# Attention 0: value product one unit later with two buffers, and each unit's last projection copied one unit later on ScalarE

## The reference

```python
def _L0_attn_ref(x, w_qkv, w_out):
    H, D, window_size = (16, 64, 32)
    xn = rms_norm(x)
    qkv = xn @ w_qkv.T
    ...
    q = apply_rope(q, cos, sin)
    k = apply_rope(k, cos, sin)
    attn = jnp.einsum('bhqd,bhkd->bhqk', q, k) * scale
    mask = (q_pos >= k_pos) & (q_pos - k_pos <= window_size)
    attn = jnp.where(mask[None, None], attn, NEG)
    attn = jax.nn.softmax(attn, axis=-1)
    out = jnp.einsum('bhqk,bhkd->bhqd', attn, v)
    ...
    return out @ w_out.T

h = _layernorm(x, axis=-1) * (1 + ca) + sa
x = x + ga * _L0_attn_ref(h, L0_attn_w_qkv, L0_attn_w_out)
```

## Time and profile before

| | us |
|---|---|
| Median of 3 runs (1296.6 to 1300.16) | 1297.09 |
| Profiled execution, first to last instruction (span) | 1295.1 |
| What lies between this span and that median | 2.0 |
| PE busy in the span | 975.8 |
| DVE busy | 805.3 |
| ACT busy | 639.2 |
| POOL busy | 430.4 |
| Attention 0's first and last y_mul, start | 121.5, 599.5 |

### The profile page before, as it was taken

One profiled execution on the slowest core, in us unless ns is written; L12 is line 12 of the kernel. 1 busy time (PEld: TensorE's weight loads), 2 busy tenths in 40 slices (PEclk: granted clock), 3 DMA queues, 4 the chain that ended last, 5 costly groups with the idle time before them and its releaser, 6 DMA issues. The chain is left out here.

```text
span 1295.1 us, 25137 instructions
## 1 busy us (share of the span) xinstructions
PE 975.8 (75%) x8604; PEld 662.5 (51%) x8604; DVE 805.3 (62%) x1683; ACT 639.2 (49%) x2132; POOL 430.4 (33%) x332
## 2 busy tenths in 40 slices
PE   6779998989899999985613769747348787867665
PEld 3456565656656565664503556534225454545454
DVE  5777758687777767564657514112136878559995
ACT  3565767767676767671101323112038777643322
POOL 2334333333342423321000857886611312200221
PEclk9789899999999998987555789888759999868967
DMA  6564343434443434431402123445310000000000
GB/s 198 150 182 107 92 123 88 119 96 113 102 113 100 113 83 107 104 91 42 102 0 62 45 59 69 61 73 129 31 66 1 1 2 1 1 1 9 17 17 25
DMA packets 89009, 93.62 MB, mean 72 GB/s; under 512 B 18800, under 2 KB 62304, under 8 KB 88944
## 3 DMA queue, kind: packets, MB, share of 16 engines
q1 hardware_dynamic: 78576, 84.12, 24.7%
q0 software_dynamic: 10368, 8.66, 4.7%
HBM read 24.36 MB, written 10.70 MB: 27 GB/s over the span
## 5 line engine op out<-in xcount | busy, mean ns | idle before, releaser
L835 POOL TENSOR_TENSOR qk_cos<-qk_raw,const 128x512 f32<-128x512 f32 x128 | 183.2, 1432 | 313.0 <-ACT qk_raw L589 313.0
L575 ACT ACTIVATE prob<-psS,neg_max 128x96 f32<-128x96 f32 x512 | 167.9, 342 | 86.5 <-DVE neg_max L670 85.7
L442 PE MATMUL psQ<-a_xnT,weights 128*128 128x512 f32 x250 | 146.0, 668 | 2.1 <-ACT a_xnT L621 1.4
L550 PEld LDWEIGHTS psO<-probT,v_windows 96*64 96x64 f32 x2048 | 73.7, 143 | 142.6 <-ACT probT L649 121.1
L550 PE MATMUL psO<-probT,v_windows 96*64 96x64 f32 x2048 | 91.8, 235 | 43.9 <-ACT probT L649 43.9
L685 DVE TENSOR_TENSOR qk_roped<-qk_cos,qk_swapped 128x512 f32<-128x512 f32 x128 | 119.0, 929 | 5.9 <-DVE qk_swapped L676 5.5
L1508 POOL DMA_INDIRECT sums<-ex_y,ex_index x64 | 97.6, 1525 | 39.5 <-issue 23.5
L1497 POOL DMA_INDIRECT ex_rows<-rows,ex_index x64 | 67.1, 1048 | 121.8 <-DMA ex_index<-lists 102.6
L575 ACT ACTIVATION_READ_ACCUMULATOR prob<-psS,neg_max 128x1 f32 x512 | 105.4, 206 | 0.0
L1442 ACT ACTIVATE ex_hidden<-ex_psH,ex_b 128x512 f32<-128x512 f32 x64 | 43.7, 687 | 114.4 <-PE ex_psH L1401 59.7
L649 ACT COPY probT<-psT 96x512 f32<-96x512 f32 x128 | 76.8, 600 | 46.5 <-PE psT L530 46.5
(11 more groups left out here) (317 smaller groups left out, 1936.2 us busy)
## 6 DMA issues: line engine op xcount, KB each, us to landing
qk_swapped<-qk_raw SPq DMA_DIRECT2D x512, 64.0 KB, 2.0
v_windows<-v_tok SPq DMA_DIRECT2D x32, 384.0 KB, 4.4
v_windows<-v_tok SPq DMA_DIRECT2D x32, 256.0 KB, 3.6
mod<-mod_rows SPq DMA_DIRECT2D x12, 512.0 KB, 6.0
ex_w<-in_L_ffn_W SPq DMA_DIRECT2D x16, 256.0 KB
v_windows<-v_tok SPq DMA_DIRECT2D x32, 96.0 KB, 2.1
...
```

The lines of the kernel that those rows point to most:

```text
L442: last = nc.tensor.matmul(bank, k.wqkvT[:, col:col + P], xnT[:, :], start=True, stop=True)
L550: ins = nc.tensor.matmul(psO[D * j:D * j + D, i * P + a * HALF:i * P + (a + 1) * HALF], vw[:, par, a, t, hd], probT[:, 2 * j + i, a * HALF ...
L575: last = nc.scalar.activation(prob[:, s, 2 * j + i, :], psS[:, s, j, i * KW:(i + 1) * KW], ACT.Exp, bias=nmax[:, s, 2 * j + i:2 * j + i + ...
L835: nc.gpsimd.tensor_tensor(rcos[:, half, :], raw[:, half, :], k.const[:, K_COS:K_COS + T], ALU.mult).then_inc(cos_done, 1)
```

## The change

PE runs O one unit late: `apply(b, u-1)` stands in unit u, before the second projection (in unit 8 before the first). probT has two buffers; O in unit u waits for the probT of unit u-1 and for the copy of the O of unit u-2. ACT copies oT of unit u-2, then probT(u), then the **last** projection of the unit before (`late`), then runs the exps, then copies the unit's other projection where it has two. v has two buffers, and the semaphore of the windows is split in two; SP issues `windows(g+1)` at t = 1 behind the swap, waiting for the value products of the quad before. The last two pairs of the output projection move into the next sequence's unit 0, behind its T, and the copy of xnT from the end of unit 7 to the middle of unit 8. The modulation weights of layer 0 use memory of mod1. DVE's and POOL's bodies are not changed.

```diff
--- before.py
+++ after.py
@@ -116,7 +116,8 @@
         sb = lambda name, shape: ctx.enter_context(nc.sbuf_tensor(f"m_{name}{layer}", shape, F32))
         sem = lambda name: ctx.enter_context(nc.semaphore(f"m_{name}{layer}"))
         self.c, self.ex, self.si, self.siT = sb("c", [B, C]), sb("exp", [B, C]), sb("silu", [B, C]), sb("siluT", [C, B])
-        self.w, self.sgn, self.mag = sb("w", [C, MODS * C]), sb("sign", [B, C]), sb("mag", [B, C])
+        self.w = sb("w", [C, MODS * C]) if layer else k.mod1[:, 0, 0:MODS, :].rearrange("p b c -> p (b c)")
+        self.sgn, self.mag = sb("sign", [B, C]), sb("mag", [B, C])
         self.rows, self.n = k.mod_rows_sb[layer], 0
         self.ld, self.exped, self.chain, self.multiplied, self.siT_ready, self.rows_ready, self.rows_stored = (
             sem(n) for n in ("ld", "exped", "chain", "multiplied", "siT", "rows", "rows_stored"))
@@ -333,9 +334,9 @@
         junk, ms, mse, rms = sb("a0_squares", [P, TILES, C]), sb("a0_ms", [P, TILES]), sb("a0_mse", [P, TILES]), sb("a0_rms", [P, TILES])
         raw, swp, rcos = (sb(n, [P, 4, T]) for n in ("qk_raw", "qk_swapped", "qk_cos"))
         qk = sb("qk_roped", [P, 2, 2, 2, T])
-        v, vw = sb("v_tok", [P, TILES, 4 * D]), sb("v_windows", [KW, 2, 2, TILES, 4 * D])
+        v, vw = sb("v_tok", [P, 2, TILES, 4 * D]), sb("v_windows", [KW, 2, 2, TILES, 4 * D])
         prob = sb("prob", [P, 2, 4, KW])
-        probT = sb("probT", [KW, 4, P])
+        probT = sb("probT", [KW, 2, 4, P])
         nmax, psum_, rsum = sb("neg_max", [P, 2, 4]), sb("prob_sum", [P, 2, 4]), sb("prob_rsum", [P, 2, 4])
         oT = sb("oT", [P, PAIRS, T])
         ymul = sb("y_mul", [P, TILES, C])
@@ -358,7 +359,7 @@
         OPENING = [(0, m) for m in (0, 1, 2, 4, 3, 5)] + ["wo0", "wo1"] + [(1, m) for m in (0, 1, 2, 4, 3, 5)]
 
         scored, turned, applied = sem("scored"), sem("turned"), sem("applied")
-        normed_ready, v_placed = sem("normed_ready"), sem("v_placed")
+        normed_ready, v_placed = sem("normed_ready"), [sem(f"v_placed{i}") for i in range(2)]
         projected, x_turned, y_ready = sem("projected"), sem("x_turned"), sem("y_ready")
         exp_done, probT_ready, oT_ready = sem("exp_done"), sem("probT_ready"), sem("oT_ready")
         piece_out, square_done, xnT_ready = sem("piece_out"), sem("square_done"), sem("xnT_ready")
@@ -489,6 +490,22 @@
                                                 stop=(p == PAIRS - 1), skip_group_check=True)
                 if last_:
                     last.then_inc(y_ready, 1)
+
+            def apply(b, u):
+
+                n, g, t = b * UNITS + u, u // TILES, u % TILES
+                wait(pe, probT_ready, n + 1)
+                wait(pe, oT_ready, n)
+                if t == 0:
+                    wait(pe, v_placed[g % 2], (b * (QUADS // 2) + g // 2 + 1) * 48)
+                for i in range(2):
+                    for a in range(2):
+                        for j in range(2):
+                            hd = slice((2 * i + j) * D, (2 * i + j + 1) * D)
+                            ins = nc.tensor.matmul(psO[D * j:D * j + D, i * P + a * HALF:i * P + (a + 1) * HALF],
+                                                   vw[:, g % 2, a, t, hd], probT[:, u % 2, 2 * j + i, a * HALF:(a + 1) * HALF],
+                                                   start=True, stop=True, skip_group_check=True)
+                ins.then_inc(applied, 1)
 
             pe.wait_ge(ld_ident, 16)
             mod.turn(pe)
@@ -519,9 +536,9 @@
             pe.wait_ge(w_act, 5)
 
             def body(b, last):
+                begins = isinstance(b, int) and b == 0
                 for u in range(UNITS):
                     g, t = divmod(u, TILES)
-                    par = g % 2
 
                     wait(pe, probT_ready, b * UNITS + u)
                     for i in range(4):
@@ -529,28 +546,22 @@
                             wait(pe, normed_ready, b * UNITS + u + 1)
                         ins = nc.tensor.transpose(psT[0:KW, i, :], prob[:, u % 2, i, :], k.ident)
                     ins.then_inc(turned, 1)
+                    if u == 0 and not begins:
+                        wait(pe, oT_ready, b * UNITS)
+                        out_project(b - 1, [PAIRS - 2, PAIRS - 1], False, True)
                     if not (last and u + 2 >= UNITS):
                         score(b, u + 2)
                     pieces = pieces_at(g, t, last)
                     if u == 0:
                         wait(pe, y_read, b)
-                    if u == 8 and not last:
-                        wait(pe, xnT_ready, b + 2)
+                    if u == 8:
+                        apply(b, u - 1)
+                        if not last:
+                            wait(pe, xnT_ready, b + 2)
                     for q, m in pieces[:1]:
                         project(b, q, m)
-
-                    wait(pe, probT_ready, b * UNITS + u + 1)
-                    wait(pe, oT_ready, b * UNITS + u)
-                    if t == 0:
-                        wait(pe, v_placed, (b * QUADS + g + 1) * 48)
-                    for i in range(2):
-                        for a in range(2):
-                            for j in range(2):
-                                hd = slice((2 * i + j) * D, (2 * i + j + 1) * D)
-                                ins = nc.tensor.matmul(psO[D * j:D * j + D, i * P + a * HALF:i * P + (a + 1) * HALF],
-                                                       vw[:, par, a, t, hd], probT[:, 2 * j + i, a * HALF:(a + 1) * HALF],
-                                                       start=True, stop=True, skip_group_check=True)
-                    ins.then_inc(applied, 1)
+                    if u not in (0, 8):
+                        apply(b, u - 1)
                     for q, m in pieces[1:]:
                         project(b, q, m)
                     if u == 7 and not last:
@@ -560,8 +571,10 @@
                 wait(pe, piece_out, b * QUADS * PIECES + made - 1)
                 wait(pe, oT_ready, b * UNITS + 3 * TILES)
                 out_project(b, list(range(PAIRS - 2)), True, False)
-                wait(pe, oT_ready, b * UNITS + UNITS)
-                out_project(b, [PAIRS - 2, PAIRS - 1], False, True)
+                apply(b, UNITS - 1)
+                if last:
+                    wait(pe, oT_ready, b * UNITS + UNITS)
+                    out_project(b, [PAIRS - 2, PAIRS - 1], False, True)
 
             turns(pe, body)
 
@@ -590,8 +603,8 @@
                 else:
                     first = 2 * VALUE.index(m)
                     if first == 0:
-                        wait(act, v_placed, (b * QUADS + q) * 48)
-                    ins = nc.scalar.copy(v[:, first:first + 2, :], bank.rearrange("p (t d) -> p t d", t=2))
+                        wait(act, v_placed[q % 2], (b * (QUADS // 2) + q // 2) * 48)
+                    ins = nc.scalar.copy(v[:, q % 2, first:first + 2, :], bank.rearrange("p (t d) -> p t d", t=2))
                 ins.then_inc(piece_out, 1)
 
             def copy_sixth(n):
@@ -641,23 +654,28 @@
                     exps(0, 1)
 
             def body(b, last):
+                late = []
                 for u in range(UNITS):
                     g, t = divmod(u, TILES)
-                    if u > 0:
-                        copy_oT(b, u - 1)
+                    if u >= 2:
+                        copy_oT(b, u - 2)
                     wait(act, turned, b * UNITS + u + 1)
-                    nc.scalar.copy(probT[:, :, :], psT[0:KW, :, :]).then_inc(probT_ready, 1)
-                    pieces = pieces_at(g, t, last)
-                    for q, m in pieces[:1]:
+                    nc.scalar.copy(probT[:, u % 2, :, :], psT[0:KW, :, :]).then_inc(probT_ready, 1)
+                    for q, m in late:
                         piece(b, q, m)
+                    if u == 8 and not last:
+                        copy_xnT(b + 1)
                     if not (last and u + 2 >= UNITS):
                         exps(b, u + 2)
-                    for q, m in pieces[1:]:
+                    pieces = pieces_at(g, t, last)
+                    for q, m in pieces[:-1]:
                         piece(b, q, m)
+                    late = pieces[-1:]
                     if u == 4 and not last:
                         squares(b + 1)
-                    if u == 7 and not last:
-                        copy_xnT(b + 1)
+                for q, m in late:
+                    piece(b, q, m)
+                copy_oT(b, UNITS - 2)
                 copy_oT(b, UNITS - 1)
 
             turns(act, body)
@@ -875,9 +893,9 @@
             def windows(q):
 
                 par = q % 2
-                sp.dma_start(vw[0:WIN, par, 0, 1:TILES, :], v[P - WIN:P, 0:TILES - 1, :]).then_inc(v_placed, 16)
-                sp.dma_start(vw[WIN:KW, par, 0, :, :], v[0:HALF, :, :]).then_inc(v_placed, 16)
-                sp.dma_start(vw[:, par, 1, :, :], v[P - KW:P, :, :]).then_inc(v_placed, 16)
```

(11 more changed lines are left out.)

## The result

The changed kernel takes 1392.84 us in the median (1383.84 to 1398.44, 4 runs), the kernel before on the same chip 1298.62: a ratio of 1.072 (95% interval 1.067 to 1.077). Slower, as predicted, but 38 us beyond the predicted 1355 and outside the range of 1308 to 1378. The ratios in this document are of fast runs alone; four medians also count one run in the chip's slower state, 1318.38 (1314.36 without it), 1379.55 (1377.81), 1366.9 and 1308.96 us.

The account below looks back on a forecast made before the run. A loop of waits between DVE and ACT in attention 0 was taken as the bound, not PE. Terms of +8.0 us in six middle sequences, +8 first and +2.5 last gave +58.5, said as 1355 us, range 1308 to 1378.

Parts of the forecast that it names:

- DVE beside POOL: Ropes that meet POOL's cosines in a middle sequence: 2.5 us gone, 1.7 new, net -0.8, bounds -3 and +3.
- the copy that leaves the front of the exps: ACT's waits for q/k projections in a middle sequence: 4.7 us at most, nothing at least, -2.3 counted.
- sines' wait for swaps: DVE's stalls for late-copied halves in nine units of a middle sequence: +9.0 us, bounds 4.4 and 11.
- end of the sequence: Output projection waits for late piece 4 (+0.9) and holds other work (+1.2): +2.1 us a sequence, bounds +1 and +3.
- Value product at nothing: PE's 4.9 us wait before the value product goes, but lies off the DVE–ACT loop, so costed at nothing.
- First sequence: Half 2 behind SP's modulation loads comes 5.7 us later; with the other units' terms, +8.
- Last sequence: Stalls of units 3, 4, 7 and 8, 4.4 us, less ACT's waits and output projection savings: net +2.5.
- A: Rival: the swaps are hidden, -1.0 us a sequence, 1290 us in all; chance 0.12.
- B: Rival: PE is the bound and its slack of 7.3 us goes in all eight sequences, 1239 us; chance 0.03.
- C: Rival: SP's windows don't hold half 2; stalls 4.4 us, +3.4 a middle sequence, 1325 us; chance 0.19.
- D: Rival: PE's granted clock falls under 0.9, each sequence loses 3.4 us, some 1378 us; chance 0.12.
- the time of issues and landings: How long SP's issues and the landings take when half 1, windows and half 2 come in one burst.

Follow-up runs that it names:

- 1282 us: The kernel before with DVE's rope behind the max in all units and POOL's cosines behind the max: 1282.41 us, ratio 0.987.

## Why the prediction came out as it did

**The direction and its mechanism held.** Copy late, swap late, sines late, and the max and exps behind them: undoing the copy takes back 74 to 78 us, and the sines wait for swaps in the middle sequences, where they never did before. Even the places are right. The costed stalls were 0.8, 1.6, 1.4, 0.9, 1.8 and 0.9 us in units 3, 4, 6, 11, 12 and 15; in an undisturbed sequence the sines wait 0.7, 1.4, 1.1, 1.0, 1.7 and 1.0 in these units. Only unit 8's 1.2 is missing: stretched sines in unit 7 brought DVE there later.

**The step that failed is the term "DVE beside POOL", forecast at -0.8 us a sequence; on the path it measures +5.6.** Three things were wrong in it. I counted only ropes, and the sines, which had not been stretched before (683 ns), took 2.9 us more, in front of the max. I gave 2.5 us back for ropes that would no longer meet a cosine. 2.3 did go, but these ropes stand behind the max, where they cost nothing: that is shown by the cosines behind the max in the kernel before. And the ropes in front of the max, charged with 1.7, took 2.7. The rows to see the first were in the prediction's own sum: a copy right behind the exps ends 0.6 later, and divide takes DVE 0.68 more before it reaches the sines.

**A second term was too small the other way:** the copy that leaves the front of the exps. ACT's waits for q/k projections fell from 4.7 us a sequence to none; 4.7 was the most that the prediction gave it. What the other terms leave for it is 4.0, where 2.3 was forecast.

An undisturbed middle sequence, term by term:

| us | forecast | measured |
|---|---|---|
| sines' wait for swaps | +9.0 | +6.8 |
| DVE beside POOL, in front of the max | -0.8 | +5.6 (sines 2.9, ropes 2.7) |
| copy leaves the front of exps, and the rest of the steps | -2.3 | -4.0 (what remains of 8.4) |
| end of the sequence | +2.1 | +2.4 |
| sum | +8.0 | +10.8 |

- *Swaps.* +6.8 is within the bounds of 4.4 and 11. It is smaller mainly because wait and meeting replace one another. With the sines' wait and their stretching, a sequence lasts 79.4 with 6.8 and 2.9, 78.3 with 3.8 and 5.2, 75.7 with 8.7 and 0.1, and 80.7 with 0 and 16.2 (15 x 1.08). The two aren't independent terms, and I had added them as such.
- *End.* Right in size; 1.13 us of it is PE's wait for piece 4, the rest the product, T and the copy of oT:

```profile
622.22 5.62 PE L488 MATMUL psQ<-weights,oT 128*128 128x128 f32 x48 [1.13 <-ACT qk_raw L602]
```

- *Value product at nothing.* Wrong by itself (+3.1 with the copies of before; 1.7 of it in unit 8), for the most part hidden in the full change, it seems because that copy no longer stands in front of the exps: the copy alone costs 9.0 and the product alone 3.1, the whole 10.8.
- *First sequence, +8 forecast, +17.6 measured.* The half behind the modulation loads waits 10.01 (5.37 in the earlier trace rows), 4.6 more where 5.7 was costed. But five other sines wait 1.6 to 2.6 us each, more than in the same units of an undisturbed sequence, and the waits for swaps up to the first y_mul are 21.0 us, 6.1 before: 14.9 of the 17.6.

```profile
94.30 0.69 DVE L694 TENSOR_TENSOR qk_swapped<-qk_swapped,const 128x512 f32<-128x512 f32 x1 [10.01 <-DMA qk_swapped<-qk_raw]
```

- *Last sequence, +2.5 forecast, +6.2 measured.* Waits for swaps 6.1 (forecast 4.4) and ropes beside cosines 1.9; y_mul's wait fell by only 0.7.
- *Not foreseen:* the disturbed sequences, 75.7 - 6 x 10.8 = 10.9 us. Against 79.4 they are 7.9 (the interruption of PE), 3.2 (slow swaps behind it) and 4.4 (slow swaps in the loop's first), together 15.6; some 4.8 of that goes off, as the first and last of the six were 3.4 and 1.4 over 68.6 before too.

The 99.5 are then 6 x 10.8 + 10.9 + 17.6 + 6.2. Against the 58.5 forecast, 16.8 are missing in the middle, 10.9 in disturbed sequences, 9.6 in the first and 3.7 in the last sequence.

**The rivals.** A (swaps hidden) fell: they wait in all sequences. B (PE is the bound) fell too: with the late product alone the kernel is slower, though PE's wait for probT is gone. But my reason against it was too simple. PE isn't full, yet it is a link in the second loop; 1282 us came from easing both. C (the windows don't hold half 2) fell: they do, though taking them away gave only 1.1 a sequence. D: the granted clock was 0.96 to 0.98 in undisturbed sequences, not under 0.9, and the one at 0.98 took 79.42 us, those at 0.96 79.44 and 79.37; a price of the clock doesn't show there. Nor is the 3.4 us that D took from the earlier trace rows shown to be the clock's: with the copy behind its own unit's exps, sequences at 1.00 and at 0.96 took 80.66 and 80.67. The disturbed ones at 0.91 and 0.93 leave it open. What the prediction named as most likely to fail, the time of issues and landings, came out right in the undisturbed sequences and too short in two of the middle six.
